# Feed-forward weights made during the gated products and kept in DRAM, and the feed-forward moved into the block of the stages before it

## What is computed

```python
x = x + xattn(layernorm(x), ...)        # reads, attention, write 1, gated products, write 2
x = x + ffn(layernorm(x), weight_q, scale, zp, bias)

# inside xattn, the part that matters here
gate = einsum('bli,oi->blo', g_in, mlp_in_w[0])      # 512 -> 2048
up   = einsum('bli,oi->blo', u_in, mlp_in_w[1])
mlp_out = silu(gate) * up
hidden_states = rat_write(hidden_states, mlp_out, ...)   # write 2

# ffn
w = (weight_q - zp[:, :, None]) * scale[:, :, None]      # groups of 32 columns, 2048 x 2048
out = x @ w.T + bias
```

## Time and profile before

| | us |
|---|---|
| median of 3 runs (2452.90 to 2456.92) | 2456.71 |
| the profiled execution's own time | 2459.1 |
| its span, first to last instruction | 2457.4 |
| gated products, first to last unit | about 1009 to 1376 |
| write 2 to the last product of its tile 15 | about 1376 to 1650 |
| first feed-forward product | 1746.7 |
| last evacuation starts | 2453.7 |

### The profile page before, as it was taken

One profiled execution on the slowest core, in us unless ns is written; L12 is line 12 of the kernel. 1 busy time (PEld: TensorE's weight loads), 2 busy tenths in 40 slices (PEclk: granted clock), 3 DMA queues, 4 the chain that ended last, 5 costly groups with the idle time before them and its releaser, 6 DMA issues. The chain is left out here.

```text
span 2457.4 us, 36655 instructions
## 1 busy us (share of the span) xinstructions
PE 2196.6 (89%) x11560; PEld 1802.1 (73%) x11560; DVE 1307.4 (53%) x1760; ACT 1061.6 (43%) x1600; POOL 959.1 (39%) x629
## 2 busy tenths in 40 slices
PE   4899958999985999799999999981599999998999
PEld 3777745666654888688788899981488888887887
DVE  4777745777745898322323277675544444444222
ACT  2444425888873787422312366663222122221111
POOL 0111115999994777200000487763322222222011
PEclk8899977999996998899999999995799999999999
DMA  3678742333325665433524487865555555554343
GB/s 131 190 245 262 233 124 62 101 103 93 103 52 179 220 230 222 148 97 104 162 82 151 163 299 289 302 256 188 181 183 173 187 184 177 182 180 171 126 142 99
DMA packets 205529, 416.03 MB, mean 169 GB/s; under 512 B 16434, under 2 KB 131890, under 8 KB 178564
## 3 DMA queue, kind: packets, MB, share of 16 engines
q1 hardware_dynamic: 205444, 414.92, 51.0%
...
## 5 line engine op out<-in xcount | busy, mean ns | idle before, releaser
L2424 PE MATMUL s_psF<-s_f_wh,s_f_xh 128*128 (+1 forms) x1024 | 400.1, 391 | 67.5 <-DVE s_f_wl L2452 67.5
L2426 PE MATMUL s_psF<-s_f_wh,s_f_xl 128*128 (+1 forms) x1024 | 399.6, 390 | 0.0
L2425 PE MATMUL s_psF<-s_f_wl,s_f_xh 128*128 (+1 forms) x1024 | 399.6, 390 | 0.0
L2436 DVE TENSOR_TENSOR s_f_xl<-s_f_xr,s_f_xh 128x2048 fp32r<-128x2048 f32 x64 | 146.7, 2292 | 423.0 <-ACT s_f_xh L2395 423.0
L967 POOL TENSOR_TENSOR s_a_pl<-s_a_pf,s_a_ph 128x1024 fp32r<-128x1024 f32 x128 | 302.0, 2391 | 22.6 <-ACT s_a_pf L932 22.5
L2424 PEld LDWEIGHTS s_psF<-s_f_wh,s_f_xh 128*128 128x128 f32 x1024 | 193.2, 189 | 108.4 <-issue 68.3
L2378 POOL TENSOR_TENSOR s_f_q<-s_f_q,s_f_sz 128x512 f32<-128x512 f32 x64 | 85.8, 1342 | 424.4 <-DVE s_f_q L2442 424.4
L877 DVE TENSOR_REDUCE s_a_mx<-s_psS 128x1 f32<-128x512 f32 (+7 forms) x256 | 185.1, 755 | 120.2 <-PE s_psS L807 119.7
L2403 ACT ACTIVATE s_f_wh<-s_f_q 128x512 f32 (+1 forms) x64 | 40.4, 632 | 445.3 <-PE s_psF L2426 398.5
L2425 PEld LDWEIGHTS s_psF<-s_f_wl,s_f_xh 128*128 128x128 f32 x1024 | 193.2, 189 | 40.1
L2426 PEld LDWEIGHTS s_psF<-s_f_wh,s_f_xl 128*128 128x128 f32 x1024 | 193.0, 188 | 40.2
...
## 6 DMA issues: line engine op xcount, KB each, us to landing
s_f_xr<-xnT SPq DMA_DIRECT2D x64, 1024.0 KB, 6.7
s_q_xt<-xT SPq DMA_DIRECT2D x16, 1024.0 KB, 7.7
s_q_xc<-xP SPq DMA_DIRECT2D x16, 1024.0 KB, 9.7
hsD<-s_q_hs SPq DMA_DIRECT2D x16, 1024.0 KB, 4.9
s_w_hin<-hsD SPq DMA_DIRECT2D x16, 1024.0 KB, 4.9
hs<-s_w_res SPq DMA_DIRECT2D x16, 1024.0 KB, 3.9
s_m_raw<-giT SPq DMA_DIRECT2D x32, 512.0 KB, 3.9
...
```

The source lines that it names most:

```text
L2424: pe.matmul(psF[p][:], xh[:, p, kt], rh, start=(kt == 0), stop=False)
L2425: pe.matmul(psF[p][:], xh[:, p, kt], rl, start=False, stop=False)
L2426: mm = pe.matmul(psF[p][:], xl[:, p, kt], rh, start=False, stop=(kt == KD - 1))
L2436: dve.tensor_tensor(xl[:, p], xr[:, p], xh[:, p], ALU.subtract).then_inc(x_lo, 1)
```

## The change

There is one block now. Three parts:

1. `build_planes`: in the gated products, in units of 3, the feed-forward's weights are made in 16 groups of 4 pieces (128x2048 at a time) and both halves stored to the DRAM tensor `wF`. SP loads `p_q` and `p_sz` of group i in unit 3i+2; DVE subtracts (unit 3i+5), multiplies (3i+6) and makes the low half (3i+7), ACT the high half (3i+6), SP stores both (3i+8). There is one `p_wh` and one `p_wl`.
2. In the gated products weights 2 and 3 are loaded, and weight 2 split, during write 1, and the first gate is taken there. Write 2's weights wait for the last `wF` store.
3. `build_ffn` is written anew, without a loop, and without making weights: two planes in SBUF, the first loaded in 8 pieces of two times 512 KB from the end of write 2's last product on (`sync_ahead`), the others in units 4 to 11 of the plane before. x 0 and x 1 are loaded and split between the last steps of write 2, and units 0 and 1 run there on PE. The rest of SP's order follows after write 2 has ended.

```diff
 def build_mlp(nc, io, k, zone, w1, planes):
...
+        def gate(act, u):
+            act.wait_ge(mm_g, u + 1)
+            if u >= 2:
+                act.wait_ge(mo_ok, u - 1)
+            act.activation(sil[:, u % 2], psG[u % 2][:], ACT.Silu).then_inc(sil_ok, 1)
...
                 hi_x(act, 2)
                 hi_x(act, 3)
+                hi_w(act, 2)
+                gate(act, 0)
...
+                if u % 3 == 2 and u // 3 < planes["groups"]:
+                    planes["load"](sp, u // 3)
+                if u % 3 == 2 and 2 <= u // 3 < planes["groups"] + 2:
+                    planes["store"](sp, u // 3 - 2)
...
+                if u % 3 == 0 and 2 <= u // 3 < planes["groups"] + 2:
+                    planes["high"](act, u // 3 - 2)
...
+                if u % 3 == 2 and 1 <= u // 3 < planes["groups"] + 1:
+                    planes["less_zero"](dve, u // 3 - 1)
+                if u % 3 == 0 and 2 <= u // 3 < planes["groups"] + 2:
+                    planes["times_scale"](dve, u // 3 - 2)
+                if u % 3 == 1 and 2 <= u // 3 < planes["groups"] + 2:
+                    planes["low"](dve, u // 3 - 2)
...
+def build_planes(nc, io, k, zone):
...
+        def load(sp, i):
+            r = i % 2
+            if i >= 2:
+                sp.wait_ge(w_lo, i - 1)
+            sp.dma_start(q[:, r], io["wq"][i * KH:(i + 1) * KH].rearrange("v p n -> p v n")).then_inc(q_in[r], 16)
+            for side, name in enumerate(("scT", "zpT")):
+                sp.dma_start(sz[:, r, side], spread(io[name][i].unsqueeze(1), GR, P // GR, H)).then_inc(sz_in[r], 16)
...
+        def high(act, i):
+            act.wait_ge(w_ok, i + 1)
+            if i:
+                act.wait_ge(w_out, 32 * i)
+            act.activation(wh[:], w[:, i % 2], ACT.Copy).then_inc(w_hi, 1)
+
+        def low(dve, i):
+            dve.wait_ge(w_hi, i + 1)
+            dve.tensor_tensor(wl[:], w[:, i % 2], wh[:], ALU.subtract).then_inc(w_lo, 1)
+
+        def store(sp, i):
+            sp.wait_ge(w_lo, i + 1)
+            for hl, part in enumerate((wh, wl)):
+                dst = io["wF"][i // KH, hl].rearrange("p (j r n) -> p r j n", j=KH, r=KH)[:, i % KH]
+                sp.dma_start(dst, part[:].bitcast(F32)).then_inc(w_out, 16)
...
+def build_ffn(nc, io, k, zone, w2):
...
+        def load_x(sp, u):
+            tile = u % TILES
+            if u < TILES:
+                sp.wait_ge(w2["t_out"], 16 * (tile + 1))
+            if u >= 2:
+                sp.wait_ge(x_lo, u - 1)
+            sp.dma_start(xr[u % 2][:].rearrange("p t j -> p (t j)"), io["xnT"][tile]).then_inc(x_in[u % 2], 16)
+
+        def load_base(sp, u):
...
+            if u >= 2:
+                sp.wait_ge(y_out[u % 2], 16 * (u // 2))
+            sp.dma_start(xb[:, u % 2], io["x3"][tile * P:(tile + 1) * P, c * H:(c + 1) * H]).then_inc(xb_in[u % 2], 16)
...
+        def sync_ahead(sp, i):
+            if i == 0:
+                sp.wait_ge(w2["ab_mm"], 2 * TILES)
+                load_x(sp, 0)
+                for piece in range(3):
+                    load_piece(sp, 0, piece)
+            if i == 1:
+                for piece in range(3, PIECES):
+                    load_piece(sp, 0, piece)
+                sp.wait_ge(w2["d_mm"], TILES)
+                load_x(sp, 1)
...
+        def sync(sp):
+            for u in range(UNITS):
+                c, tile = u // TILES, u % TILES
+                if u + 2 < UNITS:
+                    load_x(sp, u + 2)
+                if 4 <= tile < 4 + PIECES and c + 1 < C:
+                    if tile == 4 and c:
+                        sp.wait_ge(mm_ok, c * TILES)
+                    load_piece(sp, c + 1, tile - 4)
+                sp.wait_ge(y_ok, u + 1)
+                sp.dma_start(io["y"][tile * P:(tile + 1) * P, c * H:(c + 1) * H], xb[:, u % 2]).then_inc(y_out[u % 2], 16)
+                if u + 2 < UNITS:
+                    if (u + 2) % TILES == 0:
+                        load_bias(sp, c + 1)
+                    load_base(sp, u + 2)
...
+        def vector(dve):
+            for u in range(UNITS):
+                if u + 2 < UNITS:
+                    lo_x(dve, u + 2)
+                dve.wait_ge(mm_ok, u + 1)
+                dve.wait_ge(b_ok, u + 1)
+                dve.tensor_tensor(xb[:, u % 2], psF[u % 2][:], xb[:, u % 2], ALU.add).then_inc(y_ok, 1)
```

More of the change, by code:

```diff
@@ L1884, in body @@
                     evacuate(s, 3)
[L1885 removed]
+            steps(act, TILES, LAST, 2, body, LAST + 1, start=1, after=after)
         def gpsimd(pool):
@@ L2133, in sync @@
         def sync(sp, load_w2, load_y):
-            for m in range(2, 4):
-                load_weights(sp, m)
             for u in range(UNITS):
@@ L2180, in vector @@
         def vector(dve, lo_w2):
-            for m in range(2, 4):
-                lo_w(dve, m)
+            lo_w(dve, 2)
             for u in range(UNITS):
@@ L2244, in _ @@
             mlp["vector"](dve, w2["vector_ahead"])
-            w2["vector"](dve)
-def timeline(eng, end, unroll, spans, body):
-    def alive(s):
-        return frozenset(n for n, (a, c) in spans.items() if a <= s < a + c)
-    def run(reg, off, s0, slot):
-        names = alive(s0)
-        body(lambda n, back=0: Step(reg, off - spans[n][0] - back, spans[n][1]), slot, lambda n: n in names)
-    signs = [tuple(alive(s) for s in range(t, min(t + unroll, end))) for t in range(0, end, unroll)]
-    t = 0
-    while t < len(signs):
-        n = 1
-        while t and t + n < len(signs) and signs[t + n] == signs[t]:
-            n += 1
-        if n > 1:
-            with eng.Fori(0, n) as i:
-                base = i * unroll
-                for j in range(unroll):
-                    run(base, t * unroll + j, t * unroll + j, j)
-        else:
-            for j in range(len(signs[t])):
-                run(None, t * unroll + j, t * unroll + j, j)
-        t += n
```

343 lines of the change are left out of this document (152 added, 191 removed).

## The result

The changed kernel took 2702.32 us (median of 4 runs, 2696.76 to 2707.33) against 2455.77 (4 runs, 2452.90 to 2456.92) for the kernel before on the same chip: ratio 1.0998, 95% interval 1.0981 to 1.1015. The profiled execution has a span of 2698.9 us against 2457.4. PE is busy 77 us longer and the span is 241.5 us longer, so most of the loss is waiting.

A forecast was written before the change was run, and what follows sets the result against it. The prediction took PE's matmuls as the bound, except in a few holes. 2587.6 us with the stages before unchanged, plus 91 in the gated products, gave a span of 2679 and a forecast of 2678 us, range 2560 to 2790.

The forecast's parts named there:

- The start: Start of the feed-forward: unit 2 starts at 1731 instead of 1770, a gain of 39 us.
- take-over some 8 us late: Write's tail: ACT takes over its last evacuation some 8 us late, with x 0's high half ahead of it.
- The feed-forward's loop: Feed-forward: a turn of waits per unit lasts 13.55 us against 10.88 of matmuls, a loss of 163 us.
- Pieces 0.5 each, 12 us: Feed-forward: plane pieces issued behind x in 24 iterations cost 0.5 us each, 12 us.
- The line of the prediction that gives 2587.6: End of the feed-forward with the stages before unchanged: 2587.6 us, +130.
- The groups' loop: Gated products: a turn of 23.5 us per group, 7.2 over PE's 16.3, 15 turns, +100 after slack.
- 4 on average: Gated products: loads of reads or weights, in half of the units, add 4 us on average to a group's turn.
- less 8 for the banks' slack: Gated products: the two banks' slack of one and a half units takes 8 us off the groups' loss, once.
- 254 or 377 GB/s for rows of 2 KB: Gated products: a group's loads priced at 254 GB/s in 2 KB rows, its stores at the write stage's 377.
- Rival 1: Gated products and feed-forward: the groups are hidden, the feed-forward's loop is not; 2578 us, chance 0.17.
- Rivals 2 and 3: Both loops: 2, neither closes, 2400 us, chance 0.05; 3, only the groups' loop binds, 2500, chance 0.05.
- Rival 4: Feed-forward: the clock falls at PE's waits, units last 16.4 us, 177 more, 2855 us; chance 0.07.

The follow-up runs named there:

- s0: The changed kernel with nothing of the feed-forward placed inside the write; it follows when the write's last store has landed: 2699.67 us.
- f1: The changed kernel with only DVE's feed-forward order swapped, the addition for unit u before the low half of x u+2: 2519.1 us.
- f2: The changed kernel with only SP's feed-forward order changed, x u+3's load issued right behind the store of y u: 2541.97 us.
- g4: The changed kernel with only wF's DRAM layout changed, so that a group's stores have rows of 8 KB instead of 2 KB: 2694.95 us.
- g6: The changed kernel with two high-half buffers, the groups' transfers on ACT's own queue, and reads' halves one unit later: 2589.97 us.
- b_all: The changed kernel with DVE's addition first, two high-half buffers, groups on ACT's queue, later read halves, x 1 and x 2 asked for earlier: 2405.12 us.

## Why the prediction was right, point by point

- **The start** was forecast at 81 us after the write's last product and came at 79.4. As a sum the step holds. As an explanation it needs a correction: I credited the gain of 39 to loads placed inside the write. s0 shows that the placement gives 7 of the 41 us at unit 2, and nothing from unit 5 on in this kernel; the rest comes from the plane being ready in DRAM, so that 16 pieces needn't be made before the first product. The step "take-over some 8 us late", and tile 15 updated at 1694.5 instead of 1668.94, was the price of the placement, nearly as large as its gain: tile 15 is normalised from 55.2 us after the last product on, and from 29.9 on in s0.
- **The feed-forward's loop** was the largest term, and f1 and f2 confirm it from both sides: broken at one place PE runs at 10.88, shortened by 2.52 the turn is the 11.03 of the sum. "Pieces 0.5 each, 12 us" had the right total for a wrong reason: turns with a piece last 13.7, those without 13.8. What added to the 13.2 of an undisturbed turn were late landings of x and of y's stores, in both kinds of turn. So the sum of 13.55 was 0.35 high for an undisturbed turn and the additions were low by as much: that the total met the measured one (852.4 and 852.6) is partly luck. The line of the prediction that gives 2587.6 adds up to 2587.2.
- **The groups' loop** is where the forecast was 22 us short. The 19.5 us of a turn without reads is what six turns measured, and the transfers in it too (13.6 for 13.5). "4 on average" for reads was 5.0: nothing in six turns, 8.4 on average in nine, 20 in one. That is 15 us over 15 turns. The "less 8 for the banks' slack" didn't show, which is the rest. The slack of PE's banks is refilled in no turn, since every turn is longer than PE's three units; it could have been given back only once, and the trace doesn't show that it was.
- **254 or 377 GB/s for rows of 2 KB**: I laid the difference on the rows. g4 shows for the stores that row length isn't it. The old trace could have told me for the loads. Right behind the stretch at 254 it moved rows of 2 KB too, at 202 GB/s with a share of 0.55, which is 367 at full share (first line). The gated products of g6 moved 290 at 0.85, 341 at full share, and the tail of the changed kernel, mostly with the plane's loads, 401 at 1.02 (second line). That is more than my 377, and more than the 358 GB/s that the prediction quotes as a limit. What made the stretch at 254 slower stays open.

```profile
1700.00:1703.00 3.00, 0.00 (x0) 0.00 (x0) 1.34 (x2) 0.00 (x0) 1.13 (x1) 0.50 0.55 202
```
```profile
1775.00:1800.00 25.00, 14.56 (x57) 11.79 (x58) 9.82 (x11) 6.99 (x11) 8.49 (x6) 0.66 1.02 401
```

- **Rival 1** (groups hidden) failed as the fixed order said. Its argument by the mean share (under one) would have held, though: g6 hides nearly all of the groups, with the same volume, at 0.85. **Rivals 2 and 3** decided on x's landing, which was 5.4 or more in the loop. Each of them needed orders that the change didn't have; b_all is rival 2 with the orders changed. That its 2405 is so near to 2400 is partly luck: its write ends 11 us later than the rival's sum had it, and unit 2 comes 7 us sooner behind that.
- **Rival 4** (the clock falls at the waits): the mean clock was 0.97 from 1845 to 1970 and 0.96 from 1850 to 2690, nowhere near the half. But it did fall, more often than a look at the first matmul behind a hole tells. Of 58 holes from 1850 on (127 us in sum) 19 were followed by a stretch at the half clock, in six cases from the first matmul on (0.76 to 0.77 us), in the others during it or up to six matmuls later. The first unit of the kind, whose matmuls go from 0.39 to 0.63 us behind a hole of 2.16, and the stretch around it (as above, clock 0.87):

```profile
1869.36 0.47 PE L2420 MATMUL s_psF<-s_f_wh,s_f_xh 128*128 128x512 f32 x1 [2.16 <-DVE s_f_xb L2398]
...
1870.59 0.63 PE L2422 MATMUL s_psF<-s_f_wh,s_f_xl 128*128 128x512 f32 x1
```
```profile
1869.00:1882.00 13.00, 12.64 (x48) 10.08 (x48) 2.87 (x3) 1.92 (x1) 1.28 (x1) 0.87 0.35 121
```

The 19 units took PE 12.5 to 14.0 us instead of 11.15, 33 us more in sum. But behind them PE waited only 1.0 us on average for the next unit instead of 2.6, and their turns last 13.5 us (median), like the others: such a drop is hidden in the wait, as the prediction said. So the clock cost PE busy time and nearly none of the kernel's, and the chance of 0.07 was fair. Of the 77 us that PE was busy longer, the feed-forward has the larger part: 725 us from unit 2 on instead of 676. In the gated products, where holes lasted up to 19.4 us, it was 372 instead of 340, at a clock of 0.88 (0.81 from 1180 to 1244).
